# A fused graph network on one Trainium2 core: edge loads to SyncE, edge copies to ScalarE, logits to VectorE

## The reference

```
L0: three graph attention layers, 4 heads of 24:
    e   = leaky_relu(alpha_s[src] + alpha_d[dst], 0.2)
    m   = segment_max(e, dst);  ex = exp(e - m[dst])
    out = segment_sum(h[src] * ex / segment_sum(ex, dst)[dst], dst) + b;  x = relu(out)
L1: pooled = segment_sum(x[src], dst) + (1 + eps) * x;  two-layer net, batch norm, relu
L2: per-edge dot products of 4 heads, clipped, exp, normalized, weighted sum of values
L3: msg = relu(x[src] + edge_attr @ We + be);  aggr = segment_sum(msg, dst);  net, batch norm, relu
```

## Time and profile before

| what | us |
|---|---|
| median of three runs | 5864.07 |
| the profiled execution | 5863.81 |
| its span | 5862.1 |
| PE busy | 3511.6 (60%) |
| DVE busy | 3123.5 (53%) |
| ACT busy | 2625.6 (45%) |
| POOL busy | 3883.7 (66%) |
| mean granted TensorE clock | 0.777 of 2.4 GHz |

### The profile page before, as it was taken

The page is one execution under the profiler, slowest core; times in us unless marked ns, Lnnn a source line. Parts: engine busy times, 40 slices in busy tenths (PEclk is TensorE's granted clock), DMA queues, the critical chain, the costliest instruction groups (busy, mean ns, idle before and its releaser), DMA issues. The chain is left out here.

```text
span 5862.1 us, 68109 instructions
## 1 busy us (share of the span) xinstructions
PE 3511.6 (60%) x25247; PEld 2219.0 (38%) x25248; DVE 3123.5 (53%) x3383; ACT 2625.6 (45%) x4143; POOL 3883.7 (66%) x3309
## 2 busy tenths in 40 slices
PE   3211222221034699988999889997868781667764
PEld 2211111111034455555555555554433330455542
DVE  3644555554369555445555455555579992333323
ACT  1000000000023689888888789894059891222211
POOL 1888888888884577666776578773020787777772
PEclk7555555555566899999999999998989995677765
DMA  8222222222279699757997479875542332332222
GB/s 296 20 18 20 20 18 10 1 1 0 9 251 361 169 195 199 161 115 150 195 193 156 103 164 201 184 153 152 178 166 79 109 130 74 110 81 74 75 53 24
DMA packets 427191, 683.75 MB, mean 117 GB/s; under 512 B 177678, under 2 KB 272397, under 8 KB 422768
## 3 DMA queue, kind: packets, MB, share of 16 engines
q0 software_dynamic: 236096, 287.22, 31.9%
q1 hardware_dynamic: 172432, 350.48, 17.8%
q10 hardware_dynamic: 18336, 41.70, 2.1%
HBM read 540.73 MB, written 138.43 MB: 116 GB/s over the span
## 5 line engine op out<-in xcount | busy, mean ns | idle before, releaser
L330 POOL DMA_INDIRECT counts<-plcell_add,plcell_slot x806 | 1253.9, 1556 | 385.4 <-issue 223.2
L1704 POOL DMA_INDIRECT emxg<-xtab,emsrc x856 | 944.0, 1103 | 448.4 <-issue 257.8
L714 ACT ACT_TABLE_LOAD x1 | 1.3, 1283 | 1613.2 <-PE mtps L702 1613.2
L377 PE MATMUL plpsR<-plpiece,plbefore 128*128 128x500 bf16 (+1 forms) x81 | 47.1, 582 | 813.8 <-DVE plranked L507 800.6
L422 DVE TENSOR_REDUCE plnlow<-plsame 128x13 f32<-128x1664 bf16 x62 | 117.0, 1888 | 661.6 <-DMA counts<-plcell_add,plcell_slot 661.5
L1788 PE MATMUL dotbanks<-emmsg,emsame 128*128 128x96 f32 x1712 | 316.3, 344 | 237.4 <-DVE emsame L1968 230.1
L1176 ACT ACTIVATE ga1prob<-ga1psE,ga1src_fifth 128x512 f32<-128x512 f32 (+1 forms) x700 | 407.2, 680 | 81.8 <-PE ga1psE L1281 79.1
L1176 ACT ACTIVATE ga2prob<-ga2psE,ga2src_fifth 128x512 f32<-128x512 f32 (+1 forms) x700 | 407.5, 683 | 77.0 <-PE ga2psE L1281 74.1
L1176 ACT ACTIVATE ga0prob<-ga0psE,ga0src_fifth 128x512 f32<-128x512 f32 (+1 forms) x700 | 407.1, 678 | 77.7 <-PE ga0psE L1281 74.7
L1788 PEld LDWEIGHTS dotbanks<-emmsg,emsame 128*128 128x128 f32 x1712 | 287.2, 250 | 382.2 <-issue 379.5
L1281 PE MATMUL ga0psE<-ident,ga0logit 128*128 128x128 f32 x2500 | 394.5, 288 | 55.8 <-DMA ga0logit<-log_counts 32.7
(11 more groups left out here) (403 smaller groups left out, 8577.9 us busy)
## 6 DMA issues: line engine op xcount, KB each, us to landing
ga0logit<-log_counts POOLq DMA_DIRECT2D x88, 512.0 KB
ga1logit<-log_counts POOLq DMA_DIRECT2D x88, 512.0 KB
ga2logit<-log_counts POOLq DMA_DIRECT2D x88, 512.0 KB
counts<-plzeros SPq DMA_DIRECT2D x32, 1250.0 KB, 32.7
mthalf<-counts SPq DMA_DIRECT2D x50, 800.0 KB
log_counts<-mtlogs SPq DMA_DIRECT2D x25, 1600.0 KB
ginhalf<-counts SPq DMA_DIRECT2D x50, 800.0 KB
dotlogs<-log_counts ACTq DMA_DIRECT2D x25, 1600.0 KB
```

What stands on the lines that cost most here:

```text
L330: nc.gpsimd.indirect_dma_start(counts[w][:, :], bass.IndirectOffsetOnAxis(ap=cell_slot[:, g % 2, j:j + 1], axis=0), cell_add[:, g % 2, j:j ...
L377: nc.tensor.matmul(psR[:, f // RANK_BANK, 0:k * BINS], before[:], piece[:, n % 2, f:f + k, :].rearrange("p t b -> p (t b)"), start=True, s ...
L714: nc.scalar.activation(logs[:, n % OUTS, q, :], ps[:, u % 3, 0:BW], ACT.Ln, bias=tiny[:, 0:1], scale=math.e).then_inc(log_made, 1)
L1704: nc.gpsimd.indirect_dma_start(xg[:, h, t, :], None, xtab[:, :], bass.IndirectOffsetOnAxis(ap=src[:, g, t:t + 1], axis=0)).then_inc(gather ...
```

## The change

- The 128 spare cells of both tables are zeroed before everything else of the zeroing, and from one partition to one row instead of from 128 partitions.
- `edge_scatter` becomes a class. SP issues its loads (`load`), ACT makes the two copies (`join`), GpSimd only waits for the joins and scatters. The slots of all groups are loaded at once. In the table stage load and join stand at fixed pieces; in a layer a group's load stands in SP's list eight runs ahead of its first scatter, its join on ACT at unit 4 two runs ahead.
- Kept tiles: DVE clamps them as it does the added ones (`clamp_kept`), and then adds the mask (`finish_logit` becomes a plain add). ACT's `add_bias` is gone. DVE's order in a run: clamps of the added tiles, clamps of the kept, adds of the kept, then `output` or `columns` where they are due.
- SP's reloads of `mask` wait for DVE's `logit_ready` instead of ACT.

```
@@ begin, SP
                 for part, done in zip(counts, zeroed):
+                    sp.dma_start(part[NP * NP:NP * NP + P, :].rearrange("(p f) o -> p (f o)", p=1), zeros[0:1, 0:P]).then_inc(done, 16)
+                for part, done in zip(counts, zeroed):
                     v = part[0:NP * NP, :].rearrange("(p j f) o -> j p (f o)", p=P, f=ZF)
                     for j in range(ZEROS):
                         sp.dma_start(v[j], zeros[:]).then_inc(done, 16)
-                    sp.dma_start(part[NP * NP:NP * NP + P, :], zeros[:, 0:1]).then_inc(done, 16)
@@ make_tables
+        per_group = len(pieces) / moved.count
+            load_at.setdefault(int(max(i - 2, 0) * per_group), []).append(i)
+            join_at.setdefault(int(max(i - 0.5, 0) * per_group), []).append(i)
...
                         sp.dma_start(half[:, n % RING, w], ...
+                    for i in load_at.get(n, ()):
+                        moved.load(sp, i)
...
                 for n in range(len(pieces)):
+                    for i in join_at.get(n, ()):
+                        moved.join(act, i)
@@ EdgeScatter
+    def load(self, sp, i):
+        g, k = self.first + i, i % self.STAGES
+        if i == 0:
+            sp.dma_start(self.slot[:], ...).then_inc(self.slots_loaded, 16)
+            sp.wait_ge(self.feat_cleared, 1)
+        if i >= self.STAGES:
+            sp.wait_ge(self.joined, 2 * (i - self.STAGES + 1))
+        sp.dma_start(self.ends[:, k, :, :], self.edges["ends"][:, g * G:(g + 1) * G, :]).then_inc(self.loaded[k], 16)
+        sp.dma_start(rows[0:P - 1, :], self.most[:, g * G * ED:(g + 1) * G * ED]).then_inc(self.loaded[k], 16)
...
+    def join(self, act, i):
+        k = i % self.STAGES
+        act.wait_ge(self.loaded[k], 16 * sum(self.parts(n) for n in range(k, i + 1, self.STAGES)))
+        if i >= self.STAGES:
+            act.wait_ge(self.scattered[k], 16 * G * (i // self.STAGES))
+        self.nc.scalar.activation(self.stage[:, k, :, 0:ED], self.feat[:, k, :, :], ACT.Copy).then_inc(self.joined, 1)
+        self.nc.scalar.activation(self.stage[:, k, :, ED:RW], self.ends[:, k, :, :], ACT.Copy).then_inc(self.joined, 1)
+    def scatter(self, pool):
+        pool.wait_ge(self.slots_loaded, 16)
+        for i in range(self.count):
+            pool.wait_ge(self.joined, 2 * (i + 1))
+            for t in range(G):
+                self.nc.gpsimd.indirect_dma_start(self.edges["sorted"][:, :], ..., self.stage[:, k, t, :], None).then_inc(self.scattered[k], 16)
@@ gat_attend
+        LOAD_AHEAD, JOIN_AHEAD = 8, 2
+        JOIN_UNIT = 4
-        BIAS_AT = (1, 5)
+        MASK_FREE_AT = (3, 5)
...
+                def clamp_kept(r, q):
+                    if r >= L_BUFS:
+                        dve.wait_ge(turned, run_end(r - L_BUFS))
+                    nc.vector.tensor_scalar(logit[:, r % L_BUFS, q, 0:width], src_row[:, h, first:first + width], dst_bias[:, j % 2, q, h:h + 1],
+                                            low_bias[:, j % 2, q, h:h + 1], ALU.add, ALU.max).then_inc(kept_clamped, 1)
...
-                    nc.vector.scalar_tensor_tensor(part, src_row[:, h, first:first + width], least[...], part, ALU.max, ALU.add)
+                    dve.wait_ge(kept_clamped, kept_count[r] + kept_tiles(j).index(q) + 1)
+                    dve.wait_ge(mask_loaded[k], 16 * (uses + 1))
+                    nc.vector.tensor_tensor(part, part, mask[:, k, 0:width], ALU.add)
...
-                def add_bias(r, q):
-                    act.wait_ge(mask_loaded[k], 16 * (uses + 1))
-                    nc.scalar.activation(logit[...], mask[:, k, 0:width], ACT.Identity, bias=dst_bias[:, j % 2, q, h:h + 1])
...
+                    if t == JOIN_UNIT:
+                        for i in join_at.get(r, ()):
+                            moved.join(act, i)
```

More of the change, by code:

```diff
@@ L661, in make_tables @@
         pieces = [(j, k) for j in range(NB) for k in range(NB)]
-        scatter, _ = edge_scatter(nc, ctx, a, edges, "mts", *TABLE_GROUPS)
+        moved = EdgeScatter(nc, ctx, a, edges, "mts", *TABLE_GROUPS)
+        per_group = len(pieces) / moved.count
+        load_at, join_at = {}, {}
+        for i in range(moved.count):
+            load_at.setdefault(int(max(i - 2, 0) * per_group), []).append(i)
+            join_at.setdefault(int(max(i - 0.5, 0) * per_group), []).append(i)
         with nc.Block() as block:
@@ L665, in _ @@
             def _(pool):
-                for _ in scatter(pool):
+                moved.clear(pool)
+                for _ in moved.scatter(pool):
                     pass
@@ L767, in source_rows @@
     return row_kept, len(chunks)
-def edge_scatter(nc, ctx, a, edges, tag, first, last):
-    sb = lambda n, s, d=f32: ctx.enter_context(nc.sbuf_tensor(tag + n, s, d))
-    sem = lambda n: nc.alloc_semaphore(tag + n)
+class EdgeScatter:
     STAGES = 2
[L777 to L790, removed]
-        flat = a["edge_attr_32"].rearrange("e k -> (e k)")
[L792 to L820, removed]
@@ new lines, in __init__ @@
+    def __init__(self, nc, ctx, a, edges, tag, first, last):
+        sb = lambda n, s, d=f32: ctx.enter_context(nc.sbuf_tensor(tag + n, s, d))
+        sem = lambda n: nc.alloc_semaphore(tag + n)
+        self.nc, self.edges, self.first, self.count = nc, edges, first, last - first
+        self.steps = self.count * G
+        self.slot = sb("slot", [P, self.steps], i32)
+        self.ends = sb("ends", [P, self.STAGES, G, 2])
+        self.feat = sb("feat", [P, self.STAGES, G, ED])
+        self.stage = sb("stage", [P, self.STAGES, G, RW])
+        self.feat_cleared, self.slots_loaded, self.joined = (sem(n) for n in ("feat_cleared", "slots_loaded", "joined"))
+        self.loaded = [sem(f"loaded{k}") for k in range(self.STAGES)]
+        self.scattered = [sem(f"scattered{k}") for k in range(self.STAGES)]
+        flat = a["edge_attr_32"].rearrange("e k -> (e k)")
+        self.most = flat[0:(P - 1) * ET * ED].rearrange("(p f) -> p f", f=ET * ED)
+        self.rest = flat[(P - 1) * ET * ED:E * ED].rearrange("(p f) -> p f", p=1)
@@ L952, in gat_attend @@
                 i = kept_tiles(oj).index(oq)
-                loads.append((first_unit[max(r - AHEAD, 0)] + BIAS_AT[i], 1, ("mask", j, c, q, act_count[r] + i + 1)))
+                loads.append((first_unit[max(r - AHEAD, 0)] + MASK_FREE_AT[i], 1, ("mask", j, c, q, kept_count[r] + i + 1)))
+        group_run = [min(r for r in range(len(runs)) if steps_done(r) > i * G) for i in range(moved.count)]
+        join_at = {}
+        for i, r in enumerate(group_run):
+            join_at.setdefault(max(r - JOIN_AHEAD, 0), []).append(i)
+            loads.append((first_unit[r - LOAD_AHEAD] + 0.5 if r >= LOAD_AHEAD else -0.5 + i / 100, 2, ("edges", i)))
         loads.sort(key=lambda l: l[:2])
@@ L1106, in _ @@
                             clamp(r + AHEAD, q)
-                    for i in range(MOST + 1):
-                        if ahead is not None and i < len(kept_tiles(ahead)):
-                            finish_logit(r + AHEAD, kept_tiles(ahead)[i])
-                        if run == 2 and j and i == 1:
-                            output(j - 1)
+                        for q in kept_tiles(ahead):
+                            clamp_kept(r + AHEAD, q)
+                        for q in kept_tiles(ahead):
+                            finish_logit(r + AHEAD, q)
+                    if run == 2 and j:
+                        output(j - 1)
                     if run == RUNS - EARLY - 1 and j + 1 < BLOCKS:
```

64 lines of the change are left out of this document (33 added, 31 removed).

## The result

| | us |
|---|---|
| before, median of 6 runs beside it | 5865.8 |
| changed, median of 6 runs | 5917.5 |
| ratio | 1.0084, 95% interval [1.0072, 1.0097] |
| profiled execution's span | 5913.6 (before 5862.1) |

What follows compares the result with a forecast made beforehand. It took GpSimd to pace the counting stage, VectorE the table stage, and ScalarE, or PE where window sums lie, the layers. Terms -24 + 4 - 168 = -188 took 5863.8 to 5676 us, forecast 5610 to 5745, range 5590 to 5785.

Steps and rivals of the forecast that it cites:

- part 4: Attention layers, what the moved work buys: 168 us over three layers, assuming SP's queue delays later loads only by issue time.
- Rival D: Attention layers: slower, masks land late behind SP's fuller queue; at 14 us landing 5988 us; chance 0.05.
- Step 1: Counting stage: spare cells zeroed first remove dead stretches of 13 and 12 us; gain 24 (8 to 27).
- Step 2: Table stage: halves of piece 1 are issued later behind edge loads, delaying DVE's second sum; cost 4 us (0 to 12).
- Step 3: Attention layers, work moved: ScalarE falls to about 385 us, VectorE rises to 491, GpSimd falls to 415 plus 70 of gaps.
- Step 4: Attention layers: four-tile blocks gain 8 us each, blocks 0 and 5 9.5, the last 5; 56 a layer, 168 in all.
- The pace: Four-tile blocks without window sums: a group of four units goes from 3.35 towards 3.00 us, 5.7 us a block.
- the sum of waits: Attention layers: PE's waits for masks (32.7 us) and exps (17.7) shrink, by 2.3 a four-tile block and 1.3 in blocks 0 and 5.
- rival B: Attention layers: GpSimd, held off by VectorE's new clamps, or the DMA queues set the time; 5780 us; chance 0.22.
- the lockout by clamps: Attention layers: 141 us of new clamps, holding GpSimd off in full, would make it need 626 us a layer.

Runs made afterwards that it cites:

- the load split: Changed kernel with each edge group's 127-row feature load issued as rows 0 to 111 and 112 to 126: 5715.5 us, ratio 0.9766.
- edges (split): Kernel before with only the edge work moved (SyncE loads, ScalarE joins), feature load split at row 112: 5829.3 us, ratio 0.9966.
- logits: Kernel before with only the logits moved (VectorE clamps kept tiles and adds the mask, no ScalarE bias): 5880.9 us, ratio 1.0046.

## Why the prediction was wrong

Forecast -188 us, measured +52. With the load split the same change gives -142. So 194 of the 240 us of error are one cause, and 46 are sizes.

**The step that failed** is in part 4: "SP is moved nothing critical: ... so masks and joins behind them in its queue lose at most their issue time". I checked that the waits ahead of the loads were met and that an issue is short, and took the landing of a 206 KB load from GpSimd's queue to SP's as it was. On SP's queue it goes in one part instead of sixteen: 10.6 us alone, about 25 in the case above and 11 to 32 over the layers. A sixteenth of each load behind it waits for it, and the next issue is held for 11 to 14 us in the median. PE's waits for `joined` (29, 40 and 37 us) are six to seven tenths of the 50, 59 and 62 us by which a layer is longer than with the split; the rest carries no one name in the trace. Rival D was about late data behind SP's queue and had 0.05, but it named the masks and a longer landing as cause, not the rows of `joined`; PE waited for masks 24.6 us in layer 0, less than the 32.7 before.

**Step 1** (spare cells, 24): right, 25 alone; the seventh add at 113.85 against "near 113".

**Step 2** (tables, cost 4): some 36 in the changed kernel. From the last add to layer 0's first transpose it is 319.2 us with the split (1611.2 to 1930.3) and 317.7 before (1640.5 to 1958.2): 1.4 lost where 4 were forecast, so the step was near but for the failed one. DVE waits for halves 16.2 us against 13.8.

**Step 3** (durations): clamps of 0.82, measured 805 to 831 ns at width 1024; joins of 0.6 + 0.3, measured 0.54 + 0.22. The totals came out otherwise: DVE 491 forecast and 451 measured, ScalarE 385 and 424, GpSimd 415 and 477 (485 with the split). Part of it is arithmetic: an engine's busy time counts records that overlap once, so taking off a line's whole time takes off too much. GpSimd's scatters and masks alone are 436 of the 497 us, so 61 could go, not 82; the lines of ScalarE before add up to 624 of its 572. The other part is that the operations stretched. The scatters' mean rose from 1261 to 1360 ns and the mask issues' from 1080 to 1274; in busy time (measured from 1958 to 2605 before) that is 24 and 17 us, with the split 32 and 19.

**Step 4** (56 a layer): 37, 47 and 41 with the split, 42 in the mean. The three-tile blocks gave 20 of the 24 that were forecast, the four-tile blocks 22 of 32 (means of the layers). The pace was right where neither window sums nor masks interfere. Two starts of the value matmuls in a block of four tiles, with the split:

```profile
2364.48 1.06 PE L1290 MATMUL ga0psO<-ga0prob,hx 128*32 128x512 f32 x8
...
2367.49 1.06 PE L1290 MATMUL ga0psO<-ga0prob,hx 128*32 128x512 f32 x8
```

3.01 us apart, against 3.35 with a bias before and 3.00 forecast; in three-tile blocks it is 2.48. Nor is it the sum of waits that is missing: 12 us a layer were to go, and the idle time before the transposes fell from 55.8, 54.3 and 50.9 us to 45.5, 43.2 and 41.9. The mis-sized term is the pace of the four-tile blocks, where GpSimd starts two masks a run. Lines of layer 0 with the split:

```profile
L1305 PE MATMUL ga0psE<-ident,ga0logit 128*128 128x128 f32 x2500 | 370.5, 285 | 45.5 <-DMA ga0logit<-log_counts 23.5 <-issue 16.6 <-DVE ga0logit L1108 4.3
L839 POOL DMA_INDIRECT sorted_edges<-ga0sstage,ga0sslot x246 | 342.3, 1392 | 74.8 <-issue 74.8
```

PE waits 23.5 us for masks (32.7 before) and 16.6 without a named releaser (2.2); the waits for exps (17.7) are nearly gone (1.7). I read it as rival B in small: denser work on VectorE stretches GpSimd. A scatter in layer 0 with no logit operation on VectorE beside it takes 0.99 us; one that overlaps only two-tensor additions 1.74; one that overlaps only clamps 1.12 (split kernel; 83, 58 and 66 of them). Before, beside the max-and-adds alone, it took 1.31 (104). So B's doubt was partly right, but for the wrong operation: I had left the two-tensor operations as they were, and they now come two behind each other. That this order is what makes the difference is argued; no run changes it alone.

The Trainium skill ("SBUF — State Buffer", section "Who interferes with whom") has a clause that I passed over: a VectorE instruction with two inputs in SBUF contends with a GpSimd instruction that reads SBUF. GpSimd's copies (790 to 1288 ns) and scatters agree with it; of the lockout by clamps that the prediction weighed, the rows show little.

**What the sum could not show**: it added the two moves. Measured alone, spare cells, edges (split) and logits give -25, -23 and +24, together -24; in one kernel -142. About 118 us exist only when both are made. Before, ScalarE and GpSimd each filled some 88% of the layer (572 us busy; 497 and 70 of gaps; of 647); relieving either leaves the other, and the logit move loads GpSimd further. The sums of the two single moves show that they don't add; this reason for it is read from the rows.

What stays open: how much of the split kernel's 16.6 us of PE's "issue" is masks (a wait for several semaphores is put down to one), and how much of the four-tile blocks' shortfall; no run takes the masks off GpSimd.

## What to carry to other kernels

When a DMA moves from GpSimd's queue to SyncE's or ScalarE's, look at its number of rows, not only at its bytes and issue time: here 127 rows went in one part from either of those queues, and splitting them at 112 cost one more issue. A count of semaphore events at the landing tells how many parts a load had. Ask of every queue what stands behind the moved load; the stall shows at the next small DMA, not at the guilty one. Don't subtract one line's time from an engine's busy time without looking for overlaps. Where two engines stand near the bound, price the moves together and try them together: one alone may measure as nothing or as a loss.

## What the runs showed that I had not expected

- 1664-byte rows from HBM, SyncE's queue, quiet: 128 rows 2.6 to 3.5 us, 127 rows 10.6 to 10.8, 120 rows 2.6, 113 rows 9.7, 112 rows 2.3.
- A DMA of one row behind such a load is issued in 3.0 to 3.2 us instead of 0.2, and in up to 35.5 us in layer 2, where the DMA engines are 79% busy.
- The parts that end in a semaphore event at the landing: 16 for 128, 112, 64 and 16 rows, 15 for 120 and 15 rows, 1 for 127, 113 and 1.
- A load in one part slows others on other queues: with it on ScalarE's queue, masks of 512 KB on SyncE's land in 7.8 to 8.0 us instead of 5.9 to 6.4.
- GpSimd's copy of 128x416 takes 1.29 us instead of 0.79 beside denser two-tensor work on VectorE, its scatter 1.74 instead of 0.99 where it overlaps it.
